# Linear-attention megakernel on one core: attention rows turned through VectorE blocks and DRAM instead of on TensorE

## What is computed

```
q = phi(h @ wq + bq)        # phi(t) = elu(t) + 1, 16 heads of 8 features
k = phi(h @ wk + bk)
v = h @ wv + bv
kv  = einsum('bshd,bshm->bhdm', k, v)
z   = 1.0 / (einsum('bshd,bhd->bsh', q, k.sum(axis=1)) + 1e-06)
att = einsum('bshd,bhdm,bsh->bshm', q, kv, z)
h = _ln(h + att @ wo + bo, g1, be1)
y = gelu(h @ w1 + c1) @ w2 + c2
h = _ln(h + y, g2, be2)
```

## Time and profile before

| what | value |
|---|---|
| median of 3 runs | 1062.64 us (1062.22 to 1063.05) |
| the profiled execution's own time | 1060.62 us |
| its span in the profile | 1058.9 us |
| granted TensorE clock, mean | 0.98 of full |
| PE busy | 986.6 us, 93% |
| ACT, POOL, DVE busy | 79%, 79%, 74% |

### The profile page before, as it was taken

How to read it: one execution, slowest core, us unless ns; L and a number is a source line. 1 busy time by engine, 2 the same in 40 slices (tenths; PEclk the granted TensorE clock), 3 DMA queues, 4 the chain that set the end, 5 groups by cost and what they waited for, 6 DMA issues and landing times.

```text
span 1058.9 us, 24788 instructions
## 1 busy us (share of the span) xinstructions
PE 986.6 (93%) x7558; PEld 926.6 (88%) x7558; DVE 779.3 (74%) x2681; ACT 836.2 (79%) x1621; POOL 832.9 (79%) x1209
## 2 busy tenths in 40 slices
PE   5899999999999999999999999999998859989994
PEld 4799998999899989999999999999997759889993
DVE  6777777777677777777777777777788888853545
ACT  6888888888888888988888888888887646665573
POOL 5867888888888888888888888877866677677753
PEclk9999999999999999999999999999999978999997
DMA  4101263135314431453154116501302345567363
GB/s 141 51 1 56 69 158 78 56 104 123 80 58 118 126 78 60 124 131 82 61 147 98 56 61 166 98 2 41 121 1 81 96 131 166 177 192 223 96 183 130
DMA packets 101937, 106.41 MB, mean 100 GB/s; under 512 B 8716, under 2 KB 81427, under 8 KB 101680
## 3 DMA queue, kind: packets, MB, share of 16 engines
q1 hardware_dynamic: 95920, 95.32, 33.2%
q0 software_dynamic: 4544, 8.47, 2.3%
q10 hardware_dynamic: 1344, 1.05, 0.3%
HBM read 56.61 MB, written 45.17 MB: 96 GB/s over the span
## 4 chain that ended last, share of the span: by engine, by line
PE 52%; POOL 18%; DVE 10%; issue 9%; ACT 8%; DMA 2%; SPq 1%; POOLq 0%; DVEq 0%; ACTq 0%
PE psum L1962 12%; PE psum L1839 5%; PE psum L1841 5%; PE psum L1840 5%; PE psum L2121 5%; PE psum L2105 4%; ACT s L1052 4%; PE psum L1886 4%; PE psum L1892 4%; POOL rstd L771 4%; PE psum L1874 3%; POOL xt_lo L890 3%; PE psum L1920 3%; POOL res_a L821 2%; POOL res_a L814 2%
## 5 line engine op out<-in xcount | busy, mean ns | idle before, releaser
L1052 ACT ACTIVATE s<-s,shift,rstd 128x128 f32<-128x128 f32 x496 | 204.1, 487 | 45.4 <-POOL shift L773 44.5
L1962 PE MATMUL psum<-this_w,hid 128*128 128x128 f32 x1792 | 214.3, 275 | 0.0
L1962 PEld LDWEIGHTS psum<-this_w,hid 128*128 128x128 f32 x1792 | 206.9, 192 | 0.0
L1031 ACT ACTIVATE hid<-psum,col 128x512 f32<-128x512 f32 x256 | 159.4, 694 | 2.5 <-PE psum L1841 1.7
L771 POOL TENSOR_TENSOR rstd<-var,neg_half 128x4 f32<-128x4 f32 x132 | 144.3, 1093 | 11.0
L1353 DVE TENSOR_TENSOR s<-psum,res_f 128x512 f32<-128x512 f32 x64 | 44.2, 691 | 94.1 <-PE psum L1962 93.9
L1267 DVE BATCH_NORM_STATS2 stat<-s 128x6 f32<-128x128 f32 x512 | 110.2, 276 | 1.1
L1839 PE MATMUL psum<-x_hi,this_w 128*128 128x512 f32 x224 | 95.5, 426 | 1.2 <-DVE x_lo L1339 1.2
L799 POOL TENSOR_TENSOR res_f<-res_f,row 128x512 f32<-128x512 f32 x64 | 92.3, 1442 | 5.0
L2121 PE MATMUL psum<-heads,hid 128*128 x624 | 85.1, 280 | 6.8 <-ACT hid L1185 4.8
L814 POOL TENSOR_TENSOR res_a<-s,row 128x512 f32<-128x512 f32 x60 | 77.4, 1289 | 15.5 <-ACT s L1052 12.1
(11 more groups left out here) (270 smaller groups left out, 2750.6 us busy)
## 6 DMA issues: line engine op xcount, KB each, us to landing
xs<-pad SPq DMA_DIRECT2D x18, 975.0 KB, 8.8
spill<-xrow SPq DMA_DIRECT2D x26, 512.0 KB, 2.6
feature<-spill SPq DMA_DIRECT2D x104, 128.0 KB, 2.9
res_a<-w SPq DMA_DIRECT2D x28, 256.0 KB
xblk<-xs SPq DMA_DIRECT2D x78, 65.0 KB
row<-rows SPq DMA_DIRECT2D x8, 512.0 KB, 5.2
raw_w<-w SPq DMA_DIRECT2D x15, 256.0 KB, 3.9
this_w<-next_w SPq DMA_DIRECT2D x7, 512.0 KB, 3.2
```

Source lines behind the costliest of these rows:

```text
L1031: a.activation(hid[h][:, c, :], ps(3 + h + c), ACT.Gelu, bias=col[:, bass.ds(lw * FF + (C_C1 + c), 1)]).then_inc(hid_done, 1)
L1052: ins = a.activation(dst[:, t, :], src[:, t, :], ACT.Identity, bias=shift[i][:, t:t + 1], scale=rstd[i][:, t:t + 1])
L1962: ins = t_.matmul(ps(down_bank(l, s, h))[:, t * P:(t + 1) * P], hid[h][:, c, t * P:(t + 1) * P], down[:, c, :], start=c == 0, stop=c == FF ...
```

## The change

In slots 0 to 29 (`turned_late`; slots 30 and 31 stay as they were) `flip_att` and `copy_att` go. DVE's new `turn_att` transposes the 32x32 blocks of `att` behind each `attend`; SP's new `bounce` writes the 512 KB of both halves to a DRAM scratch, waits, and reads them back in four DMAs; `out_proj` takes its stationary columns from there, every eighth column (`(n h t)`), and runs in the next slot, behind that slot's project(s,0). The order in the slot is rewritten on all engines:

- PE: project(s,0), out_proj(s-1,0), out_proj(s-1,1), project(s,1), ff_down(s-2,1), flip_x1(s-1,0), key_value(s,0), key_value(s,1), attention(s,0), attention(s,1), flip_x1(s-1,1), ff_up(s-1,0), ff_up(s-1,1), ff_down(s-1,0).
- PSUM banks move: ff_down(s-2,1) goes into bank 0, where q of half 0 lies until `queries(s,0)` has read it.
- ACT does both second norms at the slot's end behind the Exp table load; POOL does both `inv_std2` ahead of `lo_moved`, and `scale_resid` and `offset_resid` of half 0 ahead of lo_moved of half 1. `bias_products` (slot 2 of a layer) and SP's loads are moved to fit.

```diff
+LATE = (LAYERS - 1) * SLOTS + 2
+def turned_late(l, s):
+    return l * SLOTS + s < LATE
...
+        def att_turned(h):
+            return att_blocks.rearrange("p (f i h t) -> p h t f i", f=QUADRANTS, h=2, t=T)[:, h]
+        def att_tile(l, s, h, k):
...
+            return att_rows.rearrange("p (n h t) -> p h t n", h=2, t=T)[:, h, k]
...
         def down_bank(l, s, h):
-            return 3 if h == 0 else 0 if l == LAST and s == 3 else 6
+            return 3 if h == 0 else 0 if (l == LAST and s == 3) or turned_late(l, s + 2) else 6
...
+            def bounce(l, s):
+                i = l * SLOTS + s
+                sp.wait_ge(attt_mm, upto(l, s, 1))
+                wait(sp, attt_sb, 16 * QUADRANTS * i)
+                sp.dma_start(att_spill.rearrange("p f c -> p (f c)"), att_blocks).then_inc(att_spilled, 16)
+                sp.wait_ge(att_spilled, 16 * i + 16)
+                wait(sp, wo_mm, upto(l, s - 1, 1))
+                for f in range(QUADRANTS):
+                    sp.dma_start(att_rows[f * BLOCK:(f + 1) * BLOCK].rearrange("p (q c) -> p q c", q=QUADRANTS),
+                                 att_spill[:, f, :].rearrange("(q j) c -> j q c", q=QUADRANTS)).then_inc(attt_sb, 16)
...
+            def turn_att(l, s, h):
+                wait(dve, att_done, upto(l, s, h))
+                wait(dve, att_spilled, 16 * (l * SLOTS + s))
+                d.transpose(att_turned(h), att[h][:, :, :].rearrange("p t (f j) -> p t f j", f=QUADRANTS)).then_inc(attt_mm, 1)
...
             def ff_down(l, s, h, between=None):
...
-                if h == 1:
+                if h == 1 and turned_late(l, s + 2):
+                    wait(pe, qt_done, upto(l, s + 2, 0))
+                elif h == 1:
                     wait(pe, s1_done, upto(l, s, 1) if l == LAST and s == 3 else upto(l, s + 1, 1))
```

More of the change, by code:

```diff
@@ L545, in layer @@
                     fill(((l - 1) * PIECES + 2) * FILL)
+                bounce(l, 2)
                 swap_blocks(l, 0)
@@ L548, in layer @@
                     set_qkv(l + 1)
[L549 to L556, removed]
+                else:
+                    set_wo(LAST)
+                    set_w2(LAST)
+                    load_end_rows()
+                bounce(l, 3)
             layer(0, 0)
@@ L930, in slot @@
                     router_constants(s)
-                if p2:
+                if s == 1 and not last:
+                    sum_rows(l + 1, 1 - ring)
+                    wait(pool, rows_summed, l * 8 + 16)
+                if late:
+                    if p2:
+                        inv_std2(l, s - 2, 0)
+                        inv_std2(l, s - 2, 1)
+                    if swapped(l, s - 3):
+                        lo_moved(l, s - 3, 0)
+                    if p2:
+                        scale_resid(l, s - 2, 0)
+                        offset_resid(l, s - 2, 0)
+                elif p2:
                     inv_std2(l, s - 2, 1)
@@ L939, in slot @@
                     resid_a(l, s - 2, 1)
[L940 to L943, removed]
+                if (s == 2 and l + 1 == LAST) or (s == 3 and l + 1 < LAST):
                     hi_w1(l + 1)
@@ L1106, in slot @@
                     norm1(l, s - 1, 1)
-                phi_k(l, s, 1)
+                if not late:
+                    phi_k(l, s, 1)
                 if last and s == 3:
@@ L1123, in slot @@
                     split_moved(l, s - 3, 0)
-                if p2:
+                if p2 and not late:
                     norm2(l, s - 2, 0)
@@ L1129, in slot @@
                     split_moved(l, s - 3, 1)
+                if late:
+                    load_table(ACT.Exp, 1, exp_table, l * SLOTS + s)
+                    if p2:
+                        norm2(l, s - 2, 0)
+                        norm2(l, s - 2, 1)
+                    if p2 and flipped(l, s - 2):
+                        split_xt(l, s - 2, 0)
+                        split_xt(l, s - 2, 1)
+                    if first and s == 0:
+                        start_split(6)
+                        start_split(7)
+                    return
                 copy_att(l, s, 0)
@@ L2009, in slot @@
                 flips2 = p2 and flipped(l, s - 2)
+                if turned_late(l, s):
+                    project(l, s, 0, first, last)
+                    if p1:
+                        out_proj(l, s - 1, 0)
+                        out_proj(l, s - 1, 1)
+                    project(l, s, 1, first, last)
+                    if first and s == 0:
+                        start(2)
+                        start(3)
+                    if p2:
+                        ff_down(l, s - 2, 1)
+                    if p1:
+                        flip_x1(l, s - 1, 0)
+                    if s == 2:
+                        bias_products(l + 1)
+                    key_value(l, s, 0)
+                    key_value(l, s, 1)
+                    attention(l, s, 0, first)
+                    attention(l, s, 1, first)
+                    if p1:
+                        flip_x1(l, s - 1, 1)
+                        ff_up(l, s - 1, 0)
+                        ff_up(l, s - 1, 1)
+                    if first and s == 0:
+                        start(4)
+                        start(5)
+                    if p1:
+                        ff_down(l, s - 1, 0)
+                    if first and s == 0:
+                        start(6)
+                        start(7)
+                    if flips2:
+                        flip_x2(l, s - 2, 0)
+                        flip_x2(l, s - 2, 1)
+                    return
                 project(l, s, 0, first, last)
+                if turned_late(l, s - 1):
+                    out_proj(l, s - 1, 0)
+                    out_proj(l, s - 1, 1)
                 project(l, s, 1, first, last)
-                if first and s == 0:
-                    start(2)
-                    start(3)
                 if p2:
@@ L2029, in slot @@
                     ff_up(l, s - 1, 1)
-                if first and s == 0:
-                    start(4)
-                    start(5)
                 flip_att(l, s, 0)
@@ L2036, in slot @@
                 flip_att(l, s, 1)
-                if s == 2 and not last:
-                    bias_products(l + 1)
                 if s == 2 and last:
```

181 lines of the change are left out of this document (140 added, 41 removed).

## The result

| | before | changed |
|---|---|---|
| median | 1062.85 us (1062.22 to 1065.31, 4 runs) | 1265.28 us (1260.03 to 1269.0, 4 runs) |
| ratio | | 1.190 (95% interval 1.185 to 1.194) |
| profiled execution, span | 1058.9 us | 1263.0 us |
| mean granted clock | 0.98 | 0.96 |

The change is slower, as forecast, but by 202 us and not by 137: the time lies 5 us above the upper end of the range.

A forecast was written before the change was run, and what follows sets the result against it. PE was taken as the bound: a slot of 24.62 us less 0.88 plus waits of 2.95, 1.07 and 0.96 makes 28.72; 28 slots add 115 us and clock falls 24 to 1060.6: 1200 us, range 1128 to 1260.

The forecast's parts named there:

- the transposes' 0.88: Eight transposes of the attention rows leave PE, saving 0.88 us a slot.
- gap 1: PE waits 2.95 us a slot ahead of ff_down(s-2,1), writing into bank 0, for DVE's queries(s,0).
- gap 2: PE waits 1.07 us a slot ahead of ff_up(s-1,1) for DVE's lo_x1 of half 1, behind both attends and turns.
- gap 3: PE waits 0.96 us a slot ahead of project(s,1) for POOL's lo_moved of half 1.
- Rival C: Not slower: the transposes go and no wait replaces them; 1036 us; decided at a 0.88 us wait before ff_down; chance 0.05.
- rival B: Only gap 1 opens, a slot of 26.69 us: 1119 us, or 1143 with half the clock falls; chance 0.15.
- the unpriced operations: 32-byte steps in turn_att's writes and out_proj's weight loads: counted at nothing, by the nearest rows 1.15 us a slot, +32.
- the loads hide as now: Lower end for out_proj's strided weight loads on PE: no extra time; the upper end was +1.71 us.
- rival A: The 32-byte steps cost: 1232 us, upper end 1259 (out_proj +1.71, each turn +0.68); chance 0.35.
- two reductions: Earlier DVE rows of 64 elements: 222 ns with adjoining fp32, 266 at a 16-byte step; the nearest price for steps.
- Half the falls, +24: PE's granted clock falls after gap 1 in half of 28 slots, 1.7 us each; ends 0 and 48 us.
- The start: The program's start, counted with the end at nothing: a few waits less and a few more.

The follow-up runs named there:

- E10: E1 with turn_att's output adjoining too, so both 32-byte steps are gone from the changed kernel and its order is untouched (wrong tokens): 1230.49 us.
- E1: The changed kernel with out_proj loading 128 adjoining columns of the bounced rows instead of every eighth (wrong tokens): 1253.08 us.
- E7: The kernel before with only out_proj's columns taken at a step of eight fp32 and two waits widened (wrong tokens): 1115.36 us.
- E2: The changed kernel with half 0's four out_proj tiles loaded at steps of 1, 2, 4 and 8 fp32 (wrong tokens): 1260.2 us, one run.
- E4: The changed kernel with DVE's lo_x1 of half 1 behind both attends and ahead of both turns: 1256.11 us.
- E3: The changed kernel with DVE's queries(s,0) moved ahead of the second keys_values and keys(s,0): 1186.47 us.
- E5: The changed kernel with the lists of DVE, POOL and ACT reordered, out_proj keeping its step of 32 bytes: 1141.36 us.
- E6: E5 with turn_att writing adjoining and ACT copying the bounced rows into order, so that out_proj takes adjoining columns: 1116.87 us.
- E8: E6 with DVE's queries(s,0) moved behind add_res1 and moments1 of half 0: 1108.5 us.
- E9: E8 without ACT's copies; four DMA reads put the rows in order in runs of 128 bytes, the write is four DMAs: 1124.81 us.

## Why the prediction was wrong

**Right, each within 0.15 us:** the transposes' 0.88, gap 1, and, shown by E10, gaps 2 and 3 at the price they were worked out for. The releasers were those named: queries, lo_x1, lo_moved. The rows of single operations before, put in the order of the changed lists, gave the waits. Rival C is out: its deciding figure was 0.88 us, and gap 1 is 2.92. So is rival B: all three gaps open in E10.

**The step that failed** is "For the sum I take the lower end, since the nearest operation for the turn is the turn itself", in the part on the unpriced operations. It put two terms at nothing, and with it failed "the loads hide as now" for out_proj, the larger of the two. Both steps of 32 bytes cost: out_proj 2.02 us a slot, each turn 0.45 (1.16 less 0.71). That is rival A, and both signs that the prediction named for it are there: out_proj takes 3.73 us (over 1.9), a turn 1.16 (over 0.9). Its size is near A's upper end, and out_proj even passed that (1.71, a doubling of the whole). In E10 the same bound is seen from the other side: with adjoining accesses the slot is 28.93, close to the 28.72 of the sum. The row to go by was the earlier trace rows; it had the right sign for another engine, at a step of 16 bytes, and I set it aside for the operation's own row without a step. It was weaker evidence than the prediction has it, though: one of its two reductions sums bf16, the other takes the maximum of fp32, so the step is not their only difference. The steps were found by E1, E7 and E10, not by these rows.

**How much of the miss it is.** By the table 28 x 1.93 = 54 of the 65 us above 1200 are in the slots, 12 at the start and the end, 2 in falls of the clock, less the 3 by which that sum is too large. Taking both steps away (E10) gave back only 35, mainly since the falls then rise from 26 to 46 us. The 30 us that E10 lies above 1200 are mainly these falls, 22 over the half, and the start.

**How the terms met.** Steps and gaps don't add up. out_proj's 2.02 swallowed gap 3 whole, as the prediction had it under the unpriced operations (0.96), and the turns' 0.90 lengthened gap 2 by 0.78. So a slot has 30.65 us and not 28.72 + 2.02 + 0.90 = 31.64.

**The clock.** Half the falls, +24, was right for the changed kernel (26) and by luck: where the slot was as forecast (E10), 23 of 28 slots had a fall, 46 us. Gap 1 is there 28 times in the changed kernel, E1, E2, E4 and E10 alike, at about 2.7 us, and the falls are in 14, 19, 18, 17 and 23 slots. Two slots of the changed kernel with the same gap 1 show as well that the gap's length alone doesn't decide. The windows view of PE, each gap and what follows it (us, busy us, granted clock, DMA share, GB/s):

```profile
493.49:496.21 2.72, 0.00 (x0) 1.00 0.96 239
496.21:499.40 3.19, 3.18 (x16) 0.54 0.23 84
525.50:528.50 3.00, 0.28 (x3) 1.00 0.71 191
528.50:531.50 3.00, 2.99 (x27) 1.00 0.55 164
```

Behind the first gap the clock is at the lower level, 1.2 GHz, for some 3 us, behind the second at 2.4 GHz. Most falls go with gap 1: in E3, E5, E6 and E8, where it is closed or short, the sum over slots is 3, 6, 3 and 2 us. But it need not be that gap. In E9, without it, the sum is 12 us, and in five of the six slots with a fall out_proj waited 1.8 to 2.8 us for its DMA, while waits of 2.2 and 2.3 us in two other slots brought none. Which of the long waits bring a fall stays open.

**The start** was counted at nothing and cost 9.5 us; 6.3 of it is out_proj in slot 1 waiting for the first bounce, with no work of a second slot to cover it.

**What stays open.** No order tried here brought the scheme below the kernel before; the best, E8, is 46 us above it. There the transposes' 0.88 us of PE are paid for by a way through DRAM that ends in front of out_proj: turn, write, read and a copy into order, of which about the last 1.1 us don't hide in most slots. Whether issuing the bounce from two queues would close that wait was not tried.

## What to carry to other kernels

Before an operation is moved to a cheaper engine, look at how its result is laid out for the next reader: here a step in a weight load, invisible in any count of instructions, cost more on PE than the transposes that went. An access pattern that no row of the profile shows should be priced by the nearest pattern, not by the operation's own row without it. And when a bank is reassigned, list what stands ahead of its last reader on that engine: one instruction of DVE, moved past three others, was worth 79 us.

## What the runs showed of the hardware that was not expected

- A weight load of 128 columns takes 0.19 us at a step of 4 bytes, 0.20 at 8, 0.31 to 0.33 at 16 and 0.33 to 0.34 at 32 (E2), and the matmuls behind it can't hide it: 3.73 us for 16 matmuls in place of 1.71.
- DVE's transposing write of 512 fp32 takes 1.16 us at a step of 32 bytes and 0.68 to 0.71 adjoining (E6, E10).
- A DMA of 128 KB in runs of 128 bytes landed in 3.4 us, against 3.0 in runs of 1 KB (E9); to issue four of them took some 2.8 us, against 1.75.
- After idle times of the same 2.7 us PE's granted clock fell in 14 of 28 slots of the changed kernel and stayed at 1.00 in the others; in E10 it fell in 23.
